# Where four weighted parts are added: on VectorE, with two TensorE transposes in place of ten accumulating ones

## What is computed

```python
q, k, v = (proj_chunk(W, b) for W, b in ((Wq, bq), (Wk, bk), (Wv, bv)))
out = _attn(q, k, v)                       # inside the segment
dil_idx = jnp.arange(0, SEG, DIL)          # SEG = 64, DIL = 4
kd, vd = k[:, :, :, dil_idx, :], v[:, :, :, dil_idx, :]
w = 1.0 / (2 * NN)                         # NN = 2, so 1/4
for off in range(1, NN + 1):
    for sign in (-1, 1):
        n = seg_ids + sign * off
        valid = (n >= 0) & (n < S)
        cross = _attn(q, kd[:, clip(n)], vd[:, clip(n)])
        out = out + jnp.where(valid, cross * w, 0.0)
return out @ Wo + bo
...
x = _layernorm(x + _L1_attn_ref(x, ...))
```

## Time and profile before

| what | value |
|---|---|
| median of 3 runs | 3060.8 us (3058.64 to 3072.15) |
| the profiled execution | 3052.98 us |
| its span | 3051.2 us |
| busy share of the span | PE 79%, PEld 54%, DVE 55%, ACT 34%, POOL 12% |
| chain that ended last | PE 58%, DVE 24%, ACT 9%, issue 4%, POOL 4% |
| mean granted TensorE clock | 0.909 of full speed |
| the eight rounds of the middle part | from 345 to 1223 us, near's part of them from 357 to 1161 us |

### The profile page before, as it was taken

The page is one execution under the profiler, slowest core; times in us unless marked ns, Lnnn a source line. Parts: engine busy times, 40 slices in busy tenths (PEclk is TensorE's granted clock), DMA queues, the critical chain, the costliest instruction groups (busy, mean ns, idle before and its releaser), DMA issues.

```text
span 3051.2 us, 49389 instructions
## 1 busy us (share of the span) xinstructions
PE 2415.3 (79%) x21152; PEld 1644.0 (54%) x21152; DVE 1689.6 (55%) x4103; ACT 1041.1 (34%) x1536; POOL 357.5 (12%) x605
## 2 busy tenths in 40 slices
PE   4665578899899987896687789777897777888788
PEld 2433367777777766665444455454554444545444
DVE  5776746656665654602477543765327753448541
ACT  4454212323222322021233443334333344434442
POOL 0111000011001100074110001110011000111000
PEclk8887679999999998997998999979899889999999
DMA  2000000000000000225600000000000000000000
GB/s 90 1 1 3 1 1 9 1 8 8 9 1 8 8 8 1 103 40 94 165 1 1 1 8 1 1 1 1 8 1 1 1 1 4 4 1 1 1 1 28
DMA packets 39341, 47.91 MB, mean 16 GB/s; under 512 B 7169, under 2 KB 36369, under 8 KB 38354
## 3 DMA queue, kind: packets, MB, share of 16 engines
q1 hardware_dynamic: 33490, 40.43, 4.5%
q0 software_dynamic: 5632, 4.33, 1.1%
HBM read 31.82 MB, written 12.91 MB: 15 GB/s over the span
## 4 chain that ended last, share of the span: by engine, by line
PE 58%; DVE 24%; ACT 9%; issue 4%; POOL 4%; DMA 1%; SPq 0%; DVEq 0%; ACTq 0%; POOLq 0%
PE banks L2608 7%; DVE wide_area L2481 4%; PE banks L1487 3%; PE banks L2805 2%; DVE wide_area L1891 2%; PE banks L2355 2%; PE banks L1452 2%; PE banks L1518 2%; PE banks L920 2%; PE banks L2364 2%; PE banks L1799 2%; PE banks L2595 2%; PE banks L2374 2%; PE banks L1784 2%; PE banks L948 2%
## 5 line engine op out<-in xcount | busy, mean ns | idle before, releaser
L2481 DVE TENSOR_REDUCE wide_area<-banks 128x8 f32<-128x2048 f32 x64 | 146.7, 2292 | 118.8 <-PE banks L2355 118.7
L2805 PE MATMUL banks<-wA 128*128 128x128 f32 x1290 | 192.2, 297 | 6.0 <-DVE spread L1406 6.0
L2805 PEld LDWEIGHTS banks<-wA 128*128 128x128 f32 x1290 | 171.9, 208 | 16.0 <-issue 8.7
L2460 ACT ACTIVATE weights<-banks 128x2048 f32<-128x2048 f32 x64 | 120.1, 1877 | 132.5 <-PE banks L2364 132.5
L1007 POOL TENSOR_TENSOR rstd<-moments,eps 128x4 f32<-128x4 f32 x56 | 11.9, 212 | 1213.7 <-DVE moments L996 1213.7
L991 DVE BATCH_NORM_STATS2 stats<-banks 128x6 f32<-128x128 f32 x208 | 50.2, 287 | 177.9 <-PE banks L959 108.1
L1891 DVE TENSOR_REDUCE wide_area<-banks 128x16 f32<-128x1024 f32 x80 | 94.3, 1218 | 38.6 <-PE banks L1784 38.0
L2268 DVE TENSOR_TENSOR weights<-banks,wC 128x1024 f32<-128x1024 f32 x64 | 76.8, 1217 | 23.0 <-PE banks L2131 22.6
L1487 PE MATMUL banks<-gates,wide_area 128*128 128x128 f32 x512 | 87.3, 322 | 0.0
L1000 DVE TENSOR_SCALAR xs<-banks,moments,rstd 128x128 f32<-128x128 f32 x208 | 70.6, 402 | 29.8 <-POOL rstd L1009 29.4
L2608 PE MATMUL banks<-wide_area,big 128*128 128x512 f32 x192 | 86.8, 593 | 0.0
(11 more groups left out here) (776 smaller groups left out, 6085.6 us busy)
## 6 DMA issues: line engine op xcount, KB each, us to landing
big<-in_wE SPq DMA_DIRECT2D x1, 4096.0 KB, 13.8
weights<-long_kernel SPq DMA_DIRECT2D x8, 512.0 KB, 7.1
conv<-wide_area SPq DMA_DIRECT2D x16, 256.0 KB, 2.8
wC<-in_wC SPq DMA_DIRECT2D x1, 3012.0 KB, 15.8
wC<-in_wG SPq DMA_DIRECT2D x1, 2971.0 KB, 19.9
big<-in_wT SPq DMA_DIRECT2D x1, 2560.0 KB, 12.7
x_all<-in_xT SPq DMA_DIRECT2D x1, 2048.0 KB, 9.4
total<-spread SPq DMA_DIRECT2D x8, 256.0 KB, 2.3
```

What stands on the lines that cost most here:

```text
L2460: act.activation(m.weights, bank[:, :, :].rearrange("p r c -> p (r c)"), ACT.Exp, scale=DK ** -0.5)\
L2481: return dve.tensor_reduce(m.peaks[:, k % 2, :, :].rearrange("p t (r c) -> p r t c", r=4)[:, :, :, SPARE[j]], m.bank[:, :, :].rearrange("p ...
L2805: pe.matmul(bank[:, 0:P], m.ident, m.ident, start=True, stop=True)
```

## The change

The three new DVE instructions per sequence add the parts: first parts 2 and 3 onto parts 0 and 1 (512 elements a partition, `dil_pairs`), then part 1 onto part 0 (256 elements, `dil_all`), then part 0 onto the local heads in `m.heads` (256 elements, `dil_sum`). Each waits for the one before it on the same engine. PE waits for the last of them in place of `dil_part3`, and turns the two tiles of `m.heads`. The number of pieces that a generator yields stays the same, so nothing else changes its place. Twice in each of eight rounds this takes eight matmuls out and puts three DVE instructions in: 128 and 48 in all.

```diff
             pe.wait_ge(*sg.done("dve", f"dil_part1_{b}", n))
             self.pause(pe, 1, f"dil_sum{b}")
-            pe.wait_ge(*sg.done("dve", f"dil_part3_{b}", n))
+            pe.wait_ge(*sg.done("dve", f"dil_sum{b}", n))
             for i in range(2):
-                out = bank[:, 0, i * P:(i + 1) * P]
-                laid(pe, out, m.heads[:, 2 * b + i, :], m.ident)
-                for g in range(SEGS):
-                    mm = pe.matmul(out, m.parts[:, i, g, :], m.ident, start=False, stop=(g == SEGS - 1), is_transpose=True)
+                mm = pe.transpose(bank[:, 0, i * P:(i + 1) * P], m.heads[:, 2 * b + i, :], m.ident)
             mm.then_inc(*sg.up("pe", f"dil_sum{b}"))
...
                                   ALU.mult).then_inc(*sg.up("dve", f"dil_part{r}_{b}"))
+            dve.wait_ge(*sg.done("dve", f"dil_part3_{b}", n))
+            dve.tensor_tensor(m.parts[:, :, 0:2, :], m.parts[:, :, 0:2, :], m.parts[:, :, 2:4, :], ALU.add).then_inc(*sg.up("dve", f"dil_pairs{b}"))
+            dve.wait_ge(*sg.done("dve", f"dil_pairs{b}", n))
+            dve.tensor_tensor(m.parts[:, :, 0, :], m.parts[:, :, 0, :], m.parts[:, :, 1, :], ALU.add).then_inc(*sg.up("dve", f"dil_all{b}"))
+            dve.wait_ge(*sg.done("dve", f"dil_all{b}", n))
+            dve.tensor_tensor(m.heads[:, 2 * b:2 * b + 2, :], m.heads[:, 2 * b:2 * b + 2, :], m.parts[:, :, 0, :], ALU.add)\
+               .then_inc(*sg.up("dve", f"dil_sum{b}"))
             yield from idle(2)
```

More of the change, by code:

```diff
@@ L1159, in __init__ @@
                                + each(G, "dil_max0_", "dil_max1_", "dil_query0_", "dil_query1_", "dil_recip", "dil_weight",
-                                      "dil_part0_", "dil_part1_", "dil_part2_", "dil_part3_"))
+                                      "dil_part0_", "dil_part1_", "dil_part2_", "dil_part3_", "dil_pairs", "dil_all", "dil_sum"))
     def local_keys(self, b, g):
```

## The result

The changed kernel takes 3092.07 us (median of 4, 3088.55 to 3107.3), the kernel before on the same chip 3060.2 us (4 runs, 3058.64 to 3072.15). The ratio is 1.0104 [1.0073, 1.0136]: slower by 1.0%, or 32 us. The forecast was 3073 us with a range up to 3088. The profiled execution took 3093.65 us, with a span of 3091.8 us and a mean granted clock of 0.896 in place of 0.909.

A forecast was written before the change was run, and what follows sets the result against it. DVE was taken as late in rounds 1 to 6's first sequence, DVE and PE nearly together in the second. Six rounds of 2.46 (14.8) - 1.1 - 1.7 = +12.0 us, median 3060.8 to 3073 us, range 3060 to 3088.

The forecast's parts named there:

- The bound: First sequence, rounds 1 to 6: DVE is late by 1.7 us against PE, so added DVE time is paid in full.
- The rival in which TensorE was the bound: All sequences: additions hidden and every removed matmul counts, 17.3 us faster, 3043.5 us; chance 0.06.
- First sequence, +1.66 a round: Rounds 1 to 6: three chained additions of 0.69, 0.43 and 0.43 us plus waits move all of DVE's queue by 1.66.
- Second sequence, +0.80: Rounds 1 to 6: additions end at 641.07, so ACT starts at 641.60 in place of 640.80, +0.80 us.
- The price of 0.04 us between waiting instructions: DVE: an instruction that waits for the one ahead starts 0.04 us after its end; three such in the chain.
- Eight matmuls: PE, each sequence: removal saves 0.88 or 1.7 us, only where PE is late; -1.7 in round 7's second sequence.
- the 0.35 us a place: Three places in rounds 0 and 7, two of them in round 0: ACT starts 0.35 us earlier, -1.1 in all.
- The clock: Rounds 0 to 7: no clock term in the sum; forecast with shifts of some us either way had chance 0.54.
- -2.05: Round 7: -0.35 us at one sequence and -1.7 us at the second sequence.
- The rival: Clock falls in new gaps before the sums, costing some 2 us a round after the second: 3085, uncovered 3091; chance 0.23.
- a cost of 0.8 us a round: Existing half-clock stretch in each steady round: moving work against it gives 0 to -0.83 us a round, -5 in six.
- The base: Profiled execution of 3052.98 us lies 7.8 under the runs' median of 3060.8, so 3065.0 profiled becomes 3073 us.

The follow-up runs named there:

- the additions alone: Kernel before plus the three additions on numbers nobody reads, ten matmuls kept and PE waiting for `dil_part3` as before: 3092.6 us, 1.0102.
- the stall filled: Eleven unread matmuls in PE's 3 us idle time ahead of far's first scores: kernel before 3047.8 us, 0.9958; changed kernel 3067.3 us, 1.0047.
- the turns alone: Kernel before with two transposes of `m.heads` in place of ten matmuls, no additions, the four parts left out: 3065.4 us, 1.0014.
- the run with GpSimd later: Changed kernel, eleven unread matmuls in far's stall, GpSimd's multiplication of far's rows waiting for the next round's first addition: 3066.1 us, 1.004.
- the filled kernels: Kernel before or changed kernel with unread matmuls in PE's idle places: 0.9958 (before, far's stall); changed 1.0047 (far's stall), 1.0032 (four places).

## Why the prediction was wrong

*The bound: right.* VectorE is what is late in the first sequence, and the additions alone cost what the whole change costs (1.0102 and 1.0104; with the stall filled 1.0014 and 1.0047). The rival in which TensorE was the bound fell with the turns alone.

*First sequence, +1.66 a round: mis-sized.* The term took 0.69 us for L1407. That is right where VectorE is alone, and GpSimd's multiplication beside it makes it 1.04. The clean rounds give +2.01, so 2.1 us more in six rounds. I did not look at what GpSimd does at this place. The sign stood in my own rows: the mean of 0.754 us for L2252 isn't a price of its form, as I took it to be, but seven instructions of 0.69 us and one of 1.19, beside two GpSimd additions:

```profile
1973.71 2.78 POOL L2228 TENSOR_TENSOR spread<-spread,wC 128x512 f32<-128x512 f32 x2 [9.67 <-ACT spread L2189]
1974.26 1.19 DVE L2252 TENSOR_TENSOR gates<-gates,outT 128x512 f32<-128x512 f32 x1
```

The Trainium skill has it ("SBUF — State Buffer", section "Who interferes with whom"): a VectorE instruction with two SBUF inputs contends with a GpSimd one that reads SBUF, and the later one blocks. The trace agrees: L1407 starts into GpSimd's instruction and ends 0.54 us behind it, L1411 ends 0.28 behind it in the run with GpSimd later, while L1403, which has one input in PSUM, keeps its 1.42.

*Second sequence, +0.80: right.* 2.75 - 2.01 = 0.74 in clean rounds, and 3.59 - 2.81 = 0.78 in the trace after, where 0.80 was forecast. The price of 0.04 us between waiting instructions held too.

*Eight matmuls: right where they count.* -0.88 in a clean round of the turns alone; in round 7's second sequence `dil_part` to ACT is 3.90 us (1183.40 to 1187.30) where it was 5.60, the forecast -1.7; in rounds 0 and 7 it is 3.84 for 4.20. In round 0 the 0.35 us a place don't reach the end of the round (436.76 and 436.70).

*The clock: the step that failed.* The forecast left out the clock: it put rounds 0 to 7 at an unchanged granted clock, a term of nothing, with 0.23 for falls. In six rounds, 23.4 us were lost where 6 x 2.75 = 16.5 is moved work: 6.9 is clock. Round 7 lost 7.9 us, with half clock for 34 us at a stretch, where I had -2.05: 10 us off. The two together are 17 us, and the larger miss by far against the 2.1 us of the first addition.

The rival named the mechanism, and three things in it were off. I gave it the smaller chance. It had the wrong place: it priced falls behind the second sequence's sums, and there one round of six has one. The others begin in the first sequence, some at the sums and some ahead of L1268, because a longer VectorE queue (or a shorter PE queue, as the turns alone show) also lengthens the idle time ahead of L1169. That half clock right behind the first sums costs little was right (101.40 us with it and 101.38 without); the same fall a few microseconds later wasn't covered. And I took the earlier trace rows as a cost of 0.8 us a round; filled, it gave 3.4 (102.07 to 98.63).

That the clock is the cause in rounds 1 to 6 is shown by the filled kernels: where the clock stays at 1.00, the rounds are as long as the moved work and the fill say. For round 7 no run isolated it. Over the fourteen profiled executions its length goes with its granted clock, from 100.4 us at 1.00 and 103.9 at 0.95 to 114.6 and 114.7 at 0.81 and 0.79. What sets off the long fall there stayed open.

*The base: right.* The median of the kernel before came out at 3060.2 us, where I had 3060.8. Moving the sum up by 7.8 us is the same as adding 12.0 to the median. The trap lies in comparing the two profiled executions: the one before had no halt in the first expert and the one after had one, which turns 32 us into 40.6. What this halt of 4 to 5 us is stayed open.

## What to carry to other kernels

Price moved work in rounds without a clock change and the clock apart from it: a kernel whose TensorE has idle places of 1 to 2 us close together can lose by the next microsecond of lateness an amount like that of the work itself (here up to 17 us of 32), and filling a single place can send the fall to a place where it costs more. Before a two-input VectorE instruction is put anywhere, look at what GpSimd does in those microseconds, since a price from rows where GpSimd was idle is a lower bound; and look at the longest of a group and not only at its mean. The cheapest gain here was in neither version of the sums: eleven unread matmuls in the one long stall, on the kernel before.

## What the hardware showed that I had not expected

- With idle times of 0.94 us ahead of L1169 and 0.74 ahead of L1268 and far's stall filled, no fall began in rounds 1 to 6; with 0.42, 1.44 and 0.74 us one came in every second round, at a cost of 5.8 us each.
- The same kind of fall cost nothing where PE had time in hand (101.40 us with it, 101.38 without), 1.3 us some 7 us later, and up to 7 us where it reached L1276.
- One fall in far's stall cost 3.4 us a round in the kernel before.
- A VectorE addition beside a GpSimd multiplication of 128x512: 0.69 us became 1.04, 0.43 became 1.15.
- A `keep_busy` matmul, shown as two, takes 0.22 us at full clock.
